# Graph kernel of two networks: the second half's tail by pairs of tiles instead of units of four

## What is computed

```python
edge_index = jnp.stack([src, dst])
x = _layernorm(x + _L0_gnn_ref(x, edge_index, ...))               # two attention layers, then @ Wu + bu
x = _layernorm(x + _L1_gnn_ref(x, edge_index, edge_type_34, ...)) # the part below

seg = edge_type * n + dst
agg = jax.ops.segment_sum(x[src], seg, num_segments=N_REL * n)
mean = agg.reshape(N_REL, n, -1) / jnp.maximum(cnt, 1.0).reshape(N_REL, n, 1)
h1 = jnp.einsum('rni,rio->no', mean, W_rel) + x @ W_root + b_rgcn
xw = h1 @ W_gcn
# then, with norm = dinv[src] * dinv[dst], the sum of xw[src] * norm over each node's edges,
# + xw * dinv^2 + b_gcn
```

## Time and profile before

| | us |
|---|---|
| runs | 3389.65, 3389.83, 3395.18 |
| median | 3389.83 |
| the profiled execution | 3394.14 |
| its span | 3392.4 |

### The profile page before, as it was taken

The page is one execution under the profiler, slowest core; times in us unless marked ns, Lnnn a source line. Parts: engine busy times, 40 slices in busy tenths (PEclk is TensorE's granted clock), DMA queues, the critical chain, the costliest instruction groups (busy, mean ns, idle before and its releaser), DMA issues.

```text
span 3392.4 us, 59839 instructions
## 1 busy us (share of the span) xinstructions
PE 3136.7 (92%) x17465; PEld 1985.6 (59%) x17465; DVE 2280.6 (67%) x4659; ACT 1439.4 (42%) x2551; POOL 1825.7 (54%) x1510
## 2 busy tenths in 40 slices
PE   6989898988999999999999999999999988677788
PEld 4544457977556666666666666666666644334445
DVE  8978888949855555565556888878888744452225
ACT  3745556736434344344244546555455521110012
POOL 3766610001666666666425665666666446676664
PEclk9989999998999999999999999999999999888899
DMA  4037632011343332342344555556555444654442
GB/s 131 2 95 230 209 98 90 1 68 54 124 133 103 133 130 100 129 137 100 124 142 158 191 175 174 199 165 200 175 174 193 155 132 129 187 182 130 130 128 91
DMA packets 241013, 458.35 MB, mean 135 GB/s; under 512 B 40228, under 2 KB 180387, under 8 KB 240918
## 3 DMA queue, kind: packets, MB, share of 16 engines
q1 hardware_dynamic: 169248, 271.42, 23.0%
q0 software_dynamic: 71280, 185.21, 19.2%
q10 hardware_dynamic: 390, 0.50, 0.0%
HBM read 302.39 MB, written 154.52 MB: 135 GB/s over the span
## 4 chain that ended last, share of the span: by engine, by line
PE 78%; DVE 7%; issue 5%; POOL 3%; another core or an unknown queue 3%; ACT 2%; DMA 1%; DVEq 0%; ACTq 0%; POOLq 0%
PE bank L2659 18%; PE bank L2662 17%; PE bank L2661 17%; PE bank L2648 6%; PE bank L2448 3%; POOL placed_dram L842 3%; PE bank L2501 2%; PE bank L2442 2%; PE bank L2636 2%; PE bank L2561 2%; PE bank L2635 2%; DVE arena L1812 2%; DVE arena L1850 2%; PE bank L2940 1%
## 5 line engine op out<-in xcount | busy, mean ns | idle before, releaser
L2659 PE MATMUL bank<-arena 128*128 128x384 f16 x3675 | 1200.0, 327 | 7.5 <-issue 6.5
L2661 PE MATMUL bank<-arena 128*128 128x384 f16 x3675 | 1199.0, 326 | 6.0 <-issue 5.9
L2662 PE MATMUL bank<-arena 128*128 128x384 f16 x3675 | 1199.2, 326 | 5.6 <-issue 5.5
L1320 ACT ACTIVATE arena<-bank,winv 128x384 f32<-128x384 f32 x700 | 396.3, 578 | 856.5 <-PE bank L2662 795.9
L2005 DVE SCALAR_TENSOR_TENSOR arena<-bank,winv,arena 128x384 f32<-128x384 f32 x525 | 317.2, 614 | 415.8 <-PE bank L2662 374.6
L2659 PEld LDWEIGHTS bank<-arena 128*128 128x128 f16 x3675 | 359.9, 98 | 255.7 <-issue 23.9
L2662 PEld LDWEIGHTS bank<-arena 128*128 128x128 f16 x3675 | 359.8, 98 | 243.6 <-issue 6.9
L2661 PEld LDWEIGHTS bank<-arena 128*128 128x128 f16 x3675 | 360.2, 98 | 239.4 <-issue 11.8
L931 POOL DMA_INDIRECT arena<-y_half,idx_now x360 | 402.8, 1119 | 164.4 <-issue 99.3
L1929 DVE SCALAR_TENSOR_TENSOR arena<-arena,wscale 128x1152 f16<-128x1152 f32 x245 | 379.9, 1586 | 147.9 <-ACT arena L1253 96.0
L945 POOL DMA_INDIRECT arena<-y_half,idx_now x360 | 354.2, 984 | 188.4 <-issue 104.3
(11 more groups left out here) (335 smaller groups left out, 4743.2 us busy)
## 6 DMA issues: line engine op xcount, KB each, us to landing
y_half<-arena SPq DMA_DIRECT2D x306, 384.0 KB
arena<-in_L_gnn_W_rel_dram SPq DMA_DIRECT2D x68, 1152.0 KB
arena<-y_half,idx_now POOLq DMA_INDIRECT x720
y_half<-arena SPq DMA_DIRECT2D x34, 294.0 KB
cT_dram<-arena SPq DMA_DIRECT2D x1, 5625.0 KB
arena<-cT_dram SPq DMA_DIRECT2D x9, 625.0 KB
arena<-in_x_dram SPq DMA_DIRECT2D x10, 384.0 KB
xu_dram<-arena SPq DMA_DIRECT2D x9, 384.0 KB
```

The source lines that it names most:

```text
L1320: nc.scalar.activation(y[half][:, :, c * CQ:(c + 1) * CQ], acc, ACT.Copy, scale=scale).then_inc(r_copied, 1)
L2659: nc.tensor.matmul(acc, h, w_hi[m - 1][:, k, :], start=fresh and k == 0, stop=False, skip_group_check=True)
L2661: nc.tensor.matmul(acc, h, w_lo[m - 1][:, k, :], start=False, stop=False, skip_group_check=True)
L2662: ins = nc.tensor.matmul(acc, l, w_hi[m - 1][:, k, :], start=False, stop=k == KH - 1, skip_group_check=True)
```

## The change

- The tail goes by pairs (PT = 2 tiles, PAIR_E = 256 edges): PAIRED = 171 pairs are used, which fill TU = 86 units of two pairs, the last one with a single pair.
- `pair_table` on VectorE, behind `spread_pads`, makes for each pair its first column (`tail_col`) and its bucket (`tail_bucket`), in `src_s`. It needs the bucket counts, which a new copy keeps in `small` during the sort.
- ScalarE's `pairs_in` replaces the index copy: for each pair it loads the column into a register and copies two columns of indices, of weights (into `w_now`) and of places (into `w_odd`). The first six units' copies stand before its last full step.
- `tail_onehot` reads `w_odd` and `w_now` at fixed columns. `tail_add` adds once a pair, `tail_sum` sums a pair into a bank, and waits for the add two pairs back.
- ROOT_UNITS is 34 instead of 38, and the count matrix's blocks come one every unit.
- VectorE's tail is six units written out, seven rounds of six and four units more; GpSimd's is seven rounds of twelve and two more. Five steps of VectorE's first-half loop are written out.

```diff
     CW = N + R
+    PT = 2
+    PAIR_E = PT * P
+    PAIRED = (E + NT * PAIR_E - 1) // PAIR_E
+    TU = cdiv(PAIRED, UT // PT)
...
+        tail_col, tail_bucket = (src_s[:, i * PAIRED:(i + 1) * PAIRED].bitcast(I32) for i in range(2))
...
-        ROOT_UNITS, ROOTS = 38, 4
+        ROOT_UNITS, ROOTS = 34, 4
         CT_UNIT = 21
-        CT_AT = [CT_UNIT + 3 * c // 2 for c in range(NT)]
+        CT_AT = [CT_UNIT + c for c in range(NT)]
...
-        REST = UNITS - ROOT_UNITS
...
+        REST = TU - ROOT_UNITS
...
-                sp.wait_ge(e_added, UNITS + CT_AT[c] + 2)
+                sp.wait_ge(e_added, UNITS + CT_AT[c] * (UT // PT) + 2)
...
-                pool.wait_ge(idx_next, V + 1)
-                for t in range(UT):
+                pool.wait_ge(idx_next, V + IDXB + 1)
...
-                    k, loaded, _ = tail_slot(i, m, c, t)
+                    k, loaded = tail_slot(c, t)[0:2]
...
+            def pairs_in(u):
+
+                for h in pairs_of(u):
+                    at = act.value_load(tail_col[0:1, u * (UT // PT) + h:u * (UT // PT) + h + 1], min_val=0, max_val=ET - PT)
+                    o, of = slice(h * PT, (h + 1) * PT), bass.ds(at, PT)
+                    nc.scalar.copy(idx_now[:, u % IDXB, o], idx_y[:, of])
+                    nc.scalar.copy(w_now[:, u % IDXB, o], w_s[:, of])
+                    ins = nc.scalar.copy(w_odd[:, u % IDXB, o], dst_s[:, of])
+                ins.then_inc(idx_next, 1)
...
             with act.Fori(0, AGG_PAIRS) as i:
                 one_step(1, i + 1, 1, i + 2, i)
+            act.wait_ge(e_sum, UNITS * UT + UT)
+            act.wait_ge(idx_next, UNITS + IDXB)
+            for u in range(IDXB):
+                pairs_in(u)
...
-            def tail_index(i, m, c):
-
-                act.wait_ge(e_sum, i * (m * UT) + ((HALVES - 1) * UNITS + c + 2) * UT)
-                next_index(i * m + (c + IDXB), c)
+            def tail_index(u):
+
+                act.wait_ge(e_sum, ((HALVES - 1) * UNITS + u + 2) * UT)
+                pairs_in(u + IDXB)
...
+            after(nc.vector.tensor_copy(small[:, 5 * NT:6 * NT], bank[6][:, NT:2 * NT]))
...
+            def pair_table():
+
+                ucount, held, first, ends, more = (small[:, i * NT:(i + 1) * NT] for i in (1, 5, 6, 7, 4))
+                after(nc.vector.tensor_scalar(smalli[:, :], held, float(PAIR_E - 1), None, ALU.add))
+                after(nc.vector.tensor_scalar(smalli[:, :], smalli[:, :], PAIR_E.bit_length() - 1, None, ALU.arith_shift_right))
+                after(nc.vector.tensor_scalar(first, smalli[:, :], 1.0, None, ALU.max))
+                after(nc.vector.tensor_tensor_scan(ends, ones[:, 0:NT], first, 0.0, ALU.mult, ALU.add))
+                after(nc.vector.scalar_tensor_tensor(more, ucount, float(UT // PT), first, ALU.mult, ALU.subtract))
+                dve.wait_ge(rel_inv_stored, 48)
+                col, to = src_s[:, 0:PAIRED], src_s[:, PAIRED:2 * PAIRED]
+                j, gap = iota[:, 0:PAIRED], typ_s[:, 0:PAIRED]
+                after(nc.vector.tensor_copy(col, j))
+                after(nc.vector.tensor_scalar(to, j, ends[:, 0:1], None, ALU.is_ge))
+                for k in range(NT - 1):
+                    if k:
+                        after(nc.vector.scalar_tensor_tensor(to, j, ends[:, k:k + 1], to, ALU.is_ge, ALU.add))
+                    after(nc.vector.tensor_scalar(gap, j, ends[:, k:k + 1], more[:, k:k + 1], ALU.is_ge, ALU.mult))
+                    after(nc.vector.tensor_tensor(col, col, gap, ALU.add))
+                after(nc.vector.tensor_scalar(tail_col, col, float(PT), None, ALU.mult))
+                after(nc.vector.tensor_copy(tail_bucket, to))
...
             spread_pads()
+            pair_table()
...
-                V, place, _ = unit(HALVES - 1, i, m, c)
-                for t in range(UT):
-                    at = bass.ds((i * m + c) * UT + t, 1)
+                V = i * m + (c + (HALVES - 1) * UNITS)
+                dve.wait_ge(idx_next, V + (IDXB + 1))
+                for t in range((UT // PT if m != TU else len(pairs_of(c))) * PT):
+                    at = slice(t, t + 1)
                     dve.wait_ge(e_sum, V * UT + (t + 1 + UT - 2 * UT))
-                    nc.vector.tensor_scalar(tail_oh[place * UT + t], iota[:, 0:P], dst_s[:, at], w_s[:, at],
+                    nc.vector.tensor_scalar(tail_oh[c % 2 * UT + t], iota[:, 0:P], w_odd[:, c % IDXB, at], w_now[:, c % IDXB, at],
                                             ALU.is_equal, ALU.mult).then_inc(e_oh, 1)
+
+            def tail_add(i, m, c, roots):
+
+                V = i * m + (c + (HALVES - 1) * UNITS)
+                for h in range(UT // PT) if m != TU else pairs_of(c):
+                    j = i * (m * (UT // PT)) + (c * (UT // PT) + h)
+                    b = dve.value_load(tail_bucket[0:1, bass.ds(j, 1)], min_val=0, max_val=NT - 1)
+                    o = bass.ds(b * CH, CH)
+                    dve.wait_ge(e_sum, V * UT + (UT + (h + 1) * PT))
+                    dve.wait_ge(e_added, j + (UNITS + 2))
+                    if roots:
+                        dve.wait_ge(root_added, roots)
+                    nc.vector.tensor_tensor(hs_flat[HALVES - 1][:, o], hs_flat[HALVES - 1][:, o], bank[SUMS + h][:, 0:CH],
+                                            ALU.add).then_inc(e_added, 1)
...
-            with dve.Fori(1, PAIRS - 1) as i:
+            for i in range(1, 6):
+                one_step(0, i, 0, i + 1, None)
+            with dve.Fori(6, PAIRS - 1) as i:
...
-                edge_add(HALVES - 1, 0, UNITS, u, roots)
+                tail_add(0, TU, u, roots)
...
-            for i in range(HK):
-                two_units(i)
-                if i == 0:
+            for u in range(ROOT_UNITS, ROOT_UNITS + 2 * HK):
+                tail_onehot(0, TU, u + 1)
+                tail_add(0, TU, u, roots)
+                if u - ROOT_UNITS == 1:
                     rows_with_rest()
-                elif i == 1:
+                elif u - ROOT_UNITS == 3:
                     rank_rows()
-                weight_low(i)
-            with dve.Fori(HK, REST // 2 - 1) as i:
-                two_units(i)
-            tail_onehot(0, 2, UNITS - 1)
-            edge_add(last, 0, 2, UNITS - 2, roots)
-            edge_add(last, 0, 2, UNITS - 1, roots)
-
-            dve.wait_ge(e_added, HALVES * UNITS + 2)
+                if (u - ROOT_UNITS) % 2:
+                    weight_low((u - ROOT_UNITS) // 2)
+            looped = (TU - 1 - ROOT_UNITS - 2 * HK) // IDXB
+            with dve.Fori(0, looped) as i:
+                for c in range(ROOT_UNITS + 2 * HK, ROOT_UNITS + 2 * HK + IDXB):
+                    tail_onehot(i, IDXB, c + 1)
+                    tail_add(i, IDXB, c, roots)
+            for u in range(ROOT_UNITS + 2 * HK + looped * IDXB, TU):
+                if u + 1 < TU:
+                    tail_onehot(0, TU, u + 1)
+                tail_add(0, TU, u, roots)
+
+            dve.wait_ge(e_added, UNITS + PAIRED + 2)
...
-            def tail_sum(i, m, c):
-
-                V, place, _ = unit(HALVES - 1, i, m, c)
-                acc = bank[SUMS + place][:, 0:CH]
-                pe.wait_ge(e_added, V + 1)
-                for t in range(UT):
-                    k, loaded, uses = tail_slot(i, m, c, t)
-                    pe.wait_ge(e_oh, (i * m + c) * UT + (t + 1))
-                    pe.wait_ge(loaded, uses * 16)
-                    nc.tensor.matmul(acc, tail_oh[place * UT + t], tail_rows[k], start=(t == 0), stop=(t == UT - 1))\
-                        .then_inc(e_sum, 1)
+            def tail_sum(u):
+
+                for h in pairs_of(u):
+                    acc = bank[SUMS + h][:, 0:CH]
+                    pe.wait_ge(e_added, UNITS + (u * (UT // PT) + h + 1))
+                    for t in range(h * PT, (h + 1) * PT):
+                        k, loaded, uses = tail_slot(u, t)
+                        pe.wait_ge(e_oh, u * UT + (t + 1))
+                        pe.wait_ge(loaded, uses * 16)
+                        nc.tensor.matmul(acc, tail_oh[u % 2 * UT + t], tail_rows[k], start=(t % PT == 0),
+                                         stop=(t % PT == PT - 1)).then_inc(e_sum, 1)
```

53 lines of the change are left out of this document (24 added, 29 removed).

## The result

The changed kernel took 3399.96 us (median of 9), the kernel before 3392.53 (9 runs beside it). The ratio is 1.002, 95% interval 1.0011 to 1.0029. I had forecast 3379 and faster, within 3362 to 3406; the time lies inside that range, but the sign was wrong, and it lies outside the 3371 to 3397 that I gave for the forecast's own mechanism. A later group of runs gave 3397.76 against 3393.97, ratio 1.0013 (1.0004 to 1.0021). So the change loses 4 to 7 us where I saw 11 gained.

What follows compares the result with a forecast made beforehand. TensorE was busy 92% of the span; GpSimd's gathers were taken to pace the tail. Terms -26.8 + 0.2 + 10.5 + 2.5 + 3 = -10.6 gave 3383.5 from 3394.1; with the median 4.3 lower, 3379 us, range 3362 to 3406.

Steps and rivals of the forecast that it cites:

- (c): Twelve pairs' copies on ScalarE ahead of its last full step stall TensorE: 10.5 us, between 3 and 14.
- cheap insertion rival: ScalarE's sequencer runs through table reads while copies drain, so the insertion costs 3 us: 3371.5 us; chance 0.15.
- (b): pair_table's about 35 small VectorE instructions, 14 us, hidden in idle time behind spread_pads: cost nothing.
- (e): VectorE's second add per unit in the tail: cycle 5.2 us in ten c_rest units, 2.5 us; elsewhere hidden.
- 26.8 us for the gathers: Saving in the tail from eighteen fewer GpSimd gathers at the measured pace of 1.488 us; low end 12.
- (g): Five first-half steps written out on VectorE: same instructions without the jump, TensorE bounds there; nothing.
- (h): Ten cT loads issued every unit instead of every one and a half; DMA share may reach 0.8; zero to 5 us.
- rival of the new loop: VectorE stands at each jump of the tail's new loop: 32 us, 3411 us; chance 0.05.
- (f): Tail sums of two tiles instead of four halve TensorE's lead over VectorE: 3 us, at most 45.
- My own sign for it: TensorE's waits for adds and VectorE's unnamed waits growing by over 30 us would show the short lead decides.
- rival on the short lead: TensorE's shorter lead in the tail costs 45 us instead of 3: 3421 us at full price; chance 0.2.
- (d): ScalarE's six copies and two value loads per tail unit, some 2 us of 5.9: hidden.

Runs made afterwards that it cites:

- sixteen tiles: Kernel before with units 86 to 89 left out of the tail, 344 tiles summed instead of 360, ROOT_UNITS 34: 3360.96 us, ratio 0.9927.
- pairs with a load each: Kernel before with sums in pairs and a value load per add: ratio 1.0034 with silent stretches (no engine signals), 0.9991 without.
- four banks: Changed kernel with pairs' sums going round four banks instead of two from unit 34 on: 3384.28 us, ratio 1.0000.
- twelve row buffers: Changed kernel with twelve row buffers for the gathers instead of sixteen, run without silent stretches: 3270.82 us, ratio 0.996.

## Why the prediction was wrong, point by point

**What was right.** The insertion (c) was put at 10.5 us and costs 10.9. Its mechanism shows in the rows as described: the twelve pairs run from 2711.94 to 2722.16, and TensorE stands once, for ScalarE's eviction.

```profile
2711.94 0.19 ACT L1318 COPY idx_now<-idx_y 128x2 int32 x1 [0.26 <-issue]
...
2722.16 0.19 ACT L1320 COPY w_odd<-dst_s 128x2 f32 x1
...
2724.12 0.48 PE L2718 MATMUL bank<-arena 128*128 128x384 f16 x1 [7.21 <-ACT arena L1340]
```

The stall is 7.2 us where I had 8.4, since a pair takes 0.80 us at the steady pace and not 1.0. The matmuls behind the gap start 0.32 us apart instead of 0.16 (the stretch has a granted clock of 0.93, before 1.00), and the rest of the 10.9, 3.7 us, stands against my 2.3. So the total is closer than its two parts. The cheap insertion rival falls.

The table (b) is hidden: VectorE's idle time ahead of the second attention layer, which was 32.44 us, is

```profile
731.50 1.46 DVE L1812 CUSTOM_DVE_ANT_0 arena<-arena 128x1250 f32<-128x1250 f32 x1 [18.07 <-ACT arena L1123]
```

The c_rest cycle (e) is 5.24 us against the 5.2 forecast and the 4.48 of the earlier trace rows, and there the second add comes 0.76 us after the first, as I had let it (from unit 34 on it comes 1.11 us after it in the median):

```profile
2963.50 0.55 DVE L2039 TENSOR_TENSOR arena<-arena,bank 128x384 f32 x1
2964.26 0.55 DVE L2039 TENSOR_TENSOR arena<-arena,bank 128x384 f32 x1 [0.21 <-DVE arena L2039]
...
2968.74 0.55 DVE L2039 TENSOR_TENSOR arena<-arena,bank 128x384 f32 x1
```

The 26.8 us for the gathers were right for the old form: sixteen tiles gave 25. The unrolled steps (g) changed nothing: from the first to the 10000th matmul of the products it is 1765.7 us in the kernel before (869.86 to 2635.54) and 1765.8 in the changed one (870.50 to 2636.35). The blocks' closer loads (h) left the DMA share at 0.69, as in the earlier trace rows.

The rival of the new loop falls too: its jumps take what the old ones took in the earlier trace rows, 56 ns, and 698 at most.

```profile
L2355 DVEq COMPARE_BRANCH  x7: 15/56/698, 3078.1 to 3303.2; - x7
```

The 7.36 us of the earlier trace rows weren't the jump's. They lie in a gap of 13.6 us without signals (3109.51 to 3123.12), in which VectorE's register instructions took 0.7 us each.

**The step that failed is (f)**, the shorter lead, taken at 3 us with an end of 45. My own sign for it came: TensorE's waits for adds and VectorE's waits without a named releaser sum to 219.6 us (112.6 + 107.0) against 146.7 (20.4 + 126.3), 73 more, where 30 were to decide. The gathers took 526.0 us where I had written 505 to 512. As for the price, pairs with a load each measured 11.5 us in the old kernel, against 5.5 for (e) and (f) together. With one load they measured 5 (2 to 8), so half of the 11.5 or more may be the second load's, and no run prices the lead alone. The rival on the short lead named the mechanism and a threshold of 14 us, and I gave it 0.2. What spoke against it in my text was "those are only 5 waits": TensorE rarely waited for adds before. I read the number of such waits as fixed and the lead as what each would cost. The count went from 5 waits to 43, and GpSimd's stops from 70 us to 87, with fewer gathers. That the lead sets how soon all come to a stop in a silent stretch is theory A, which the runs support in direction (stops of 74 and 83 us with pairs in the old kernel, 80 with four banks) and not in size.

**The second failure is how I read the long waits.** I took them to come with the sums, so with the units, and priced each removed gather at the mean pace that holds them. They were a feature of where the run was made: of 534 us of the old tail, 70 are GpSimd's stops, and in the traces of the other kind there are none but those that an edit made. The price held all the same in the old form, 25 us for sixteen tiles, but that run was made in the kind in which the rows were read; in the other a gather takes 1.26 us. In the changed kernel the stops grew while the units became fewer.

**Two smaller ones.** ScalarE's added work (d), put at nothing, measured 2.7 us with an interval that reaches 0. And the upper end of the forecast's own range was summed wrongly: -12 + 0.2 + 14 + 2.5 + 3 + 5 is 12.7 over 3389.8, so 3402 and not 3397; the 5 us of the loads were left out. That 3400 lies inside the stated 3362 to 3406 is owed to the room left for the rivals, not to the mechanism.

**What stays open.** Tiles -28 (18 x 1.55), insertion +10.9, pairs +11.5, ScalarE's work +2.7 add up to -3, and the changed kernel measures +4 to +7. So of the 15 to 18 us between my -10.6 and the measurement, the excess of the pairs explains 6 and ScalarE's work some 3. Each term has an interval of 3 to 5 us, so 7 to 10 us may be noise or an effect of the parts together. Four banks got 4 to 7 of it back in one group and 2 in another, less than the theory wanted. In the profiled pair 5.6 us stand behind the last gather, and no run was made for them. What starts a silent stretch is open too, and whether the stretches themselves or something else of that kind slows the pairs.

## What to carry to other kernels

A change that lets one engine run less far ahead of another may cost nothing while every signal is prompt and something when signals come late (here -3 us and +11.5 for one kernel); the number of waits in the old trace doesn't price it, since that number changes with the lead. When several engines wait in a trace with no named releaser and resume together, find out whether that belongs to the kernel before a saving is priced at a pace that contains it: the same kernel on another chip or at another time is the cheapest test. Setup work put ahead of a stretch in which TensorE is full belongs behind single evictions, a little at a time; it was worth 11 us here, more than any other edit that leaves the work as it is.

## What the runs showed of the hardware

The same kernel before takes 3285 us in two groups of runs and 3386 to 3394 in the other four, 3% apart, with all runs of a group within 0.5%. Of the 129 us between the spans of the two profiles of the pairs' kernel (3407.8 and 3278.7), 83 lie in the tail's gathers (545 and 463 us), 12 behind the last gather and 35 in the first 460 us, where rows are gathered too. In the slower kind no engine's signal comes through for 2.5 us to over 13 us at a time in the tail, while gathers follow one another every 1.25 us. In all 31 stretches counted in the changed kernel GpSimd had stopped by the end and started its next gather 0.8 to 1.0 us behind it, and in 22 of them the signals came within 0.1 us of a gather's landing, where there were several sums' 40 ns apart. GpSimd's own issue isn't affected (0.946 us a gather in the median in both kinds), and landings go on all through the stretches. VectorE's sequencer is: over the tail, 13 of its register instructions took 0.60 to 0.76 us in the kernel before, 28 in the pairs' kernel with two loads and 57 in the changed one, and none did in the faster traces of the pairs' kernel and of the twelve row buffers (median of all, 57 to 69 ns).

The Trainium skill ("Perfetto Trace Analysis", Tensor Engine Instruction (MATMUL, LD_WEIGHTS)) says that a matmul's recorded end is computed and that its signal is sent only after PSUM has acknowledged the data. The trace agrees that the two are different things: outside the tail the signal stands 13 ns behind the recorded end in the median, in the faster kind in the tail 14 ns, and in the silent stretch shown above 4.1 us.

A gather lands 3.0 to 3.1 us after its issue (median, in the runs without silent stretches), where I had read 2.7 in the tail. With a wait for the one two back, the next starts 0.77 us after that landing in the median. Two gathers then take 3.05 + 0.77 = 3.8 us, 1.9 each, near the measured 2.0 and not my 1.35, which left the second term out.
